# First kernel row of a grouped convolution by full taps in images 2 to 9, the other two rows in stacked quarters

## The reference, cut to what matters

```python
x = x + conv3x3(group_norm(x), W)              # 16 images 28x28x128, 32 groups of 4 channels, padding SAME
x = x + attention(group_norm(x), w_qkv, ...)   # neighbourhood attention, 7x7 windows, 16 heads of 8
```

## Time and profile before

| | us |
|---|---|
| median of 3 runs | 1047.03 |
| lowest and highest of the 3 | 1044.67, 1051.82 |
| the profiled execution's own time | 1053.87 |
| its span on the core | 1052.0 |
| mean granted clock of TensorE in it | 0.886 |
| PE busy, DVE busy, ACT busy | 945.5, 806.7, 657.0 |

### The profile page before, as it was taken

How to read it: one execution, slowest core, us unless ns; L and a number is a source line. 1 busy time by engine, 2 the same in 40 slices (tenths; PEclk the granted TensorE clock), 3 DMA queues, 4 the chain that set the end, 5 groups by cost and what they waited for, 6 DMA issues and landing times.

```text
span 1052.0 us, 41726 instructions
## 1 busy us (share of the span) xinstructions
PE 945.5 (90%) x16657; PEld 628.9 (60%) x16657; DVE 806.7 (77%) x2109; ACT 657.0 (62%) x1822; POOL 483.5 (46%) x842
## 2 busy tenths in 40 slices
PE   5989998779999999999898989899999998999976
PEld 3645432236667666666666666666666766676653
DVE  4487766448888888887878797888878887888864
ACT  2211244127777777867686868586868776777553
POOL 7000004046465555646474747374646464646422
PEclk9965557869999899999999999899989998999896
DMA  9785458864475756575656557565737473746421
GB/s 245 178 213 135 109 153 270 238 188 147 116 209 133 213 129 204 152 204 151 171 159 166 167 156 196 142 182 143 225 97 219 106 230 94 227 123 195 112 71 39
DMA packets 128736, 173.63 MB, mean 165 GB/s; under 512 B 31560, under 2 KB 107944, under 8 KB 125216
## 3 DMA queue, kind: packets, MB, share of 16 engines
q1 hardware_dynamic: 123200, 155.19, 53.6%
q10 hardware_dynamic: 4096, 11.73, 4.5%
q0 software_dynamic: 1248, 4.05, 1.3%
HBM read 83.65 MB, written 67.55 MB: 144 GB/s over the span
## 4 chain that ended last, share of the span: by engine, by line
PE 65%; DVE 12%; ACT 8%; issue 8%; DMA 4%; ACTq 1%; POOL 1%; SPq 1%; DVEq 0%; POOLq 0%
PE PS L1485 13%; PE PS L1524 10%; PE PS L1508 8%; PE PS L1413 7%; PE PS L1430 7%; PE PS L1501 6%; PE PS L1467 5%; DVE area L1223 3%; ACT area L861 3%; DVE S L1244 3%; ACT S L953 2%; PE PS L1418 2%; DMA area<-padded 2%; PE PS L1447 2%; DVE masked L1255 2%
## 5 line engine op out<-in xcount | busy, mean ns | idle before, releaser
L740 POOL TENSOR_TENSOR late<-masked 128x48 f32<-128x48 f32 (+1 forms) x512 | 153.0, 300 | 372.7 <-DVE masked L1255 361.1
L953 ACT ACTIVATE S<-S 128x384 f32<-128x384 f32 (+1 forms) x512 | 282.7, 554 | 30.3 <-DVE S L1244 27.0
L1485 PE MATMUL PS<-area 97*128 97x48 bf16 (+1 forms) x4096 | 250.3, 208 | 41.0 <-DVE S L1244 35.9
L1244 DVE TENSOR_TENSOR S<-PS,bias 128x384 f32<-128x384 f32 (+1 forms) x512 | 282.7, 552 | 2.7 <-PE PS L1485 0.6
L1234 DVE TENSOR_REDUCE mcol<-PS 128x6 bf16<-128x480 f32 (+2 forms) x288 | 176.2, 612 | 124.2 <-PE PS L1508 124.2
L946 ACT ACTIVATE VT<-PS 128x128 f32<-128x128 f32 x448 | 132.0, 295 | 180.1 <-PE PS L1467 176.5
L1485 PEld LDWEIGHTS PS<-area 97*128 97x128 bf16 x4096 | 178.9, 102 | 90.0 <-DVE S L1244 45.5
L1524 PE MATMUL PS<-S,VT 128*18 128x48 f32 x8192 | 196.9, 216 | 7.2 <-issue 4.9
L1524 PEld LDWEIGHTS PS<-S,VT 128*18 128x18 f32 x8192 | 117.6, 100 | 130.3 <-issue 66.7
L1508 PEld LDWEIGHTS PS<-area 128*128 128x128 bf16 x1568 | 144.8, 156 | 20.5 <-issue 6.1
L1467 PE MATMUL PS<-cst,area 128*128 128x128 f32 x448 | 142.4, 318 | 11.6 <-ACT VT L946 11.4
(11 more groups left out here) (105 smaller groups left out, 1015.3 us busy)
## 6 DMA issues: line engine op xcount, KB each, us to landing
area<-k_parts SPq DMA_DIRECT2D x32, 1008.0 KB, 7.1
area<-q_parts SPq DMA_DIRECT2D x64, 294.0 KB, 8.1
k_parts<-area SPq DMA_DIRECT2D x32, 504.0 KB, 8.0
k_parts<-area SPq DMA_DIRECT2D x32, 336.0 KB, 3.9
q_parts<-area SPq DMA_DIRECT2D x32, 294.0 KB, 7.4
out<-area SPq DMA_DIRECT2D x18, 392.0 KB, 4.2
late<-x_mid SPq DMA_DIRECT2D x17, 392.0 KB, 5.2
area<-padded ACTq DMA_DIRECT2D x19, 336.8 KB, 5.6
```

The lines of the kernel that those rows point to most:

```text
L740: nc.gpsimd.tensor_tensor(sel[:, c % SEL_RING, :, :, t0:t0 + count], m[:, :, 0], m[:, :, 1], ALU.add).then_inc(s["summed"], 1)
L953: nc.scalar.activation(S[:, n % 4, 0:cols], S[:, n % 4, 0:cols], ACT.Exp).then_inc(s["probs"], 1)
L1244: nc.vector.tensor_tensor(S[:, n % 4, 0:cols], PS[:, SCORE + n % 2, 0:cols], bias[:, at:at + cols], ALU.add).then_inc(s["biased"], 1)
L1485: last = mm(PS[:, SCORE + n % 2, cols * g:cols * (g + 1)], key_rows[a][0:PEAK_ROW + 1, g, key:key + 128], query_rows[a][0:PEAK_ROW + 1, :, ...
```

## The change

In images 2 to 9 kernel row 0 is done by full taps from the padded image, kernel rows 1 and 2 stay in stacked quarters. Images 0 and 1 (full taps) and 10 to 15 (quarters alone) are as before. The wait for the copies moves in images 2 to 9 from ahead of row 0 to ahead of row 1, and row 0 waits for the padded image. No transfer, and no instruction of another engine, is added or taken away.

```diff
+        LAST_MIXED = 9
@@ convolve(h, row)
                 m, half = divmod(h, 2)
                 to, first = PS[:, h % 2, 0:HALF], row + HALF_ROWS * half
-                if row == 0:
-                    if stacked(m):
+                if stacked(m):
+                    if row == (1 if m <= LAST_MIXED else 0):
                         pe.wait_ge(s[f"copies_in{m % 2}"], 64 * (m // 2))
                         pe.wait_ge(s["wstack_ready"], 1)
-                    else:
+                if row == 0:
+                    if m <= LAST_MIXED or not stacked(m):
                         pe.wait_ge(s["padded_ready"], m + 1)
                         pe.wait_ge(s["wconv_ready"], 1)
                     if h > 1:
                         pe.wait_ge(s["conv_added"], h - 1)
-                if stacked(m):
+                if stacked(m) and (row or m > LAST_MIXED):
                     for t in range(4):
                         ...
```

## The result

| | before | after |
|---|---|---|
| median, us (20 runs each, one set of measurements) | 1051.62 | 1040.12 |
| lowest and highest | 1044.67, 1068.07 | 1031.06, 1045.76 |
| ratio, 95% interval | | 0.9872 [0.9845, 0.9898] |
| span of the profiled execution | 1052.0 | 1029.5 |
| mean granted clock in it | 0.886 | 0.936 |

The kernel became 1.3% faster: 13.5 us by the ratio, while the medians lie 11.5 us apart. In two further sets of measurements, on chips 15 and 1, the ratio was 0.9862 [0.9797, 0.9926] and 0.9825 [0.9791, 0.9859]. The ratios, and the medians given for experiments, leave out single executions that ran in a slower state of the chip. So the profile must be read by stage, and we need more than one.

The account below looks back on a forecast made before the run. PE at its lower clock bounds halves 7 to 16, DVE next. DVE's waits for picks 14.4 + 0.85 + 0.7 - 3.3 = 12.7, about 13 us saved from 1047.03, gives 1034 us, range 1029 to 1043.

Parts of the forecast that it names:

- The bound and the next bound: Halves 7 to 16: PE at clock 0.50 bounds them, 74.7 us; DVE is next, needing 60.3 us.
- What brings the clock up: Halves 7 to 16: full 128x128 matmuls raise PE's clock, quarters never did there; upper clock for most of the stage.
- The clock falling back: Halves 7 to 16: four falls after PE's pauses, 0.8 us of DVE waiting each, 3.3 us lost (bounds 0 and 13).
- PE's slack: Halves 7 to 16: PE at the upper clock needs 5.2 us a half against DVE's 6.0, pausing about 0.8 us.
- Halves 17 to 19: After half 16: DVE's 0.85 us wait for turned patches goes, and key to query projection saves 0.7 us.
- uncovered: Half after the query projection: row 0's 1.23 us is hidden beside ACT's evacuation and casts; if not, it costs 1.2 us.
- The 7.0 us: Key to query projection if the clock has fallen in PE's pause ahead: 2.95 + 2.6 + 1.5, 1.0 us lost.
- Copies in images 2 to 9: Moved wait in images 2 to 9: copies land in time, covered by 2.5 us at the worst.
- The added 1.23 us in halves 4 to 6: Before the ten halves: PE pauses enough to take in 1.23 us a half, so 0 change.
- The low clock: Rival: clock stays low, row 0 costs 2.59 us more in halves 7 to 19; +34 us, 1081; chance 0.07.
- the copies: Rival: copies or ACT become the bound, 1 us an image in eight images; saving 5 to 6, 1041; chance 0.06.
- The swinging clock: Rival: a quarter of the ten halves run low, 9 us back; saving 5, 1042; chance 0.12.

Follow-up runs that it names:

- the mixed kernels: Changed kernel and its variants with row 0 by full taps in images 2 to 9 or beyond; ten halves 59.5 to 59.6 us where the clock didn't fall.
- the added row: Kernel before, with row 0 of images 2 to 9 first computed by full taps and thrown away; ratio 0.9915, ten halves 63.3 us.
- the two light kernels: Changed kernel and kernel before, each without the second of three DVE additions in `keep_unit`; ten halves 56.6 us (changed) and 74.3 us (before).
- the first and third profile: Two of three profiles of the changed kernel, nothing altered between them; ten halves 62.5 and 62.6 us, attention 815.3 and 825.5 us.
- POOL late: Changed kernel with POOL's two clearings of the value buffers made to wait until image 0 is normalized; ratios 0.9844 and 0.9833.
- the added-quarters kernel: Kernel before, with row 0 of images 2 to 9 computed twice by stacked quarters; ten halves 75.3 us at clock 0.65.

## Why the prediction was right, point by point

The forecast was 1034 us for a median of 1047.03, 13 us saved (1.2%); measured were 0.9872, 13.5 us of 1051.62 (11.5 between the medians), and 1040.12 lies in the range. Of the 6 us that 1040 is above 1034, 4.6 are the base: a median of three runs stood for one of twenty. The way to the saving was right in the large term and wrong in small ones.

- The bound and the next bound. PE at the lower clock, DVE behind it at 60.3 us for ten halves: the profiles of the mixed kernels with no fall of the clock give 59.5 to 59.6. Shown by the added row and by the two light kernels.
- What brings the clock up. "The quarters of the ten halves never raised it" holds for the kernel before; that quarters can, was to be seen in the same trace near 222 us. The change needed only that full taps do more, and they do.
- The clock falling back, four falls for 3.3 us (four times 0.8 is 3.2). There were two in the first and third profile, 62.5 - 59.6 = 2.9 us, 1.5 us each, and none in the second. The sum fits by luck, its terms less: fewer falls, each dearer. PE's slack was 0.3 us a half (6.0 - 5.7) and not 0.8, which fits the dearer falls. In one of them row 0 alone takes 3.76 us:

```profile
119.51 0.77 PE PS L1449 x24
120.29 3.76 PE PS L1420 x6
```

- Halves 17 to 19, 0.85 + 0.7 = 1.55 us saved. This step failed: 0.9 to 3.7 us were lost to the addition of half 19 (to the padding of image 11 from 2.6 lost to 0.2 saved). The two terms themselves came where nothing disturbed them: 0.81 and 0.65 us with POOL late. What the forecast had wrong is three things. It let DVE's slot 17 keep its length: POOL's clearing is released by the end of half 17 on PE, which moved ahead by more than DVE did, and it cost 0.8 to 1.9 us. It put row 0 of half 19 at nothing, "hidden" behind ACT: it cost 1.5 us up to the addition (the forecast has 1.2 for the case "uncovered") and 0.4 up to the padding. And in two of three profiles the clock fell ahead of row 0, after PE had waited 3.07 us for the image in the first and 2.00 in the second; the third waited 2.00 us too and had no fall. The 7.0 us that I had kept as the bound for a fallen clock came in number, but not in the way it was added up: it had the projections low (2.95) and row 0 nearly up, the trace has the projections up and row 0 low:

```profile
139.32 1.57 PE PS L1432 x4
140.89 3.65 PE PS L1420 x6
...
146.35 1.51 PE PS L1432 x4
```

- Copies in images 2 to 9 never made PE wait: in the changed kernel its waits for them begin at image 11, as before. The added 1.23 us in halves 4 to 6 was hidden (addition of half 6 at 71.15 for 70.84).
- Later stages untouched: 61.5 us for 63.3 in halves 20 to 31, much the same in all three profiles. Of these 1.8 us some 1.1 are where the cut lies (padding of image 11 comes 0.2 us after the addition of half 19 in before, 0.9 ahead of it in after); 0.6 to 0.8 are a gain that wasn't forecast, and its cause wasn't tried.
- The sum. Forecast for the first part: 14.4 - 3.3 + 1.55 = 12.7. Measured in it: 153.5 - 143.1 = 10.4, then 14.3 and 13.2 in the other two profiles. By stage that is 12.3 - 3.7 + 1.8, then 15.2 - 2.6 + 1.7 and 12.1 - 0.9 + 1.9, for a forecast of 11.1 + 1.55 + 0. Errors of 1 to 5 us with both signs stand behind a sum that is right to 1 or 2, so its closeness is luck; the mechanism is not.
- The rivals. The low clock and the copies didn't happen. The swinging clock did in a small part: some 10% of the ten halves' time in the first and third profile (two falls), not a quarter.

## What to carry to other kernels

Where PE is busy throughout and the clock row says 0.50, look at the kinds of matmul before their number: here replacing a cheap kernel row by a dearer one of full 128x128 matmuls, and even adding it on top, made the stage of ten halves 11 to 15 us shorter. The gain ends at the next engine, so work out that engine's own need (busy time plus waits for other engines than PE), and take it as the floor. When one engine gets faster, ask of every queue that waits for it, POOL's too, what will now start beside what.

## What the runs showed that I had not expected

- Stacked quarters can raise the clock as well: in the added-quarters kernel at 102 and 136 us, after two of seven equal runs of them, and in the kernel before near 222 us. With transposes and picks among them they didn't in 92 us of the kernel before (62 to 154 us).
- A memset of POOL held two casts and a normalization of DVE up by 1.9 us in one execution (2.9 us for 1.0 without it) and by 0.8 in two others of the same kernel.
- The attention stage of one and the same kernel took 815 to 826 us, and of kernels equal in it 815 to 833. A profile's total is no measure of a change of 1%; its stages are.
